# Second-group streaming in a gated attention and feed-forward block: 512-token first-layer products, tile-by-tile second layer, new call order

## The chip, the cores and the metric

The kernel runs on one core of one Trainium2 chip, in one launch. The metric is device microseconds (us). The kernel before takes 255.28 us, the median of three runs (255.18, 255.28 and 256.24). The core has a matrix engine (PE, with its weight loads shown apart as PEld), a vector engine (DVE), an activation engine (ACT), a general engine (POOL) and a queue engine (SP) that here only issues DMAs. Each engine works through its own list of instructions in order and waits on semaphores that other engines raise.

## The reference

Input x has 4 batches of 1024 tokens of 256 numbers; each batch has 154 context rows of 256. In short:

```python
xn     = layernorm(x)
scores = (xn @ Wq.T + bq) @ (ctx @ Wk.T + bk).T / 16
keep the 32 largest scores of each token, softmax over these
x  = x + tanh(g_xattn) * ((attn @ (ctx @ Wv.T + bv)) @ Wo.T + bo)
h  = relu(layernorm(x) @ W1 + b1)                # 256 -> 1024
x  = x + tanh(g_ffn) * (h @ W2 + b2)             # 1024 -> 256
```

## The kernel before, in words

Raw engine programs with semaphores written by hand. The 4096 tokens are cut into 8 groups (`GROUPS`) of 512 tokens; a group is 4 tiles of 128 tokens, and a tile pair p is two of them. Each engine has a list of calls in an order that is written out by hand (groups 0 to 2), and then a loop over g that repeats one pattern.

Setup folds Wk with Wq (`fold_queries`, `centre_queries`, `make_keys`) and Wv with Wo (`fold_values`, `values_of`), so that one product gives the scores and one the attended values. Per group and pair: `scores` (PE, plain fp32), `scale_scores` (DVE), four `topk_round` calls of eight maxima each (DVE), `exps` (ACT), `pick` (DVE), `transpose_picked` (PE), `pt_to_hi` (ACT), `pt_to_lo` (DVE), `attend` (PE), `residual` (DVE, makes x2 and its statistics), `normalise_x2` (POOL), `transpose_x2n` (PE), `x2nt_to_hi` (ACT), `x2nt_to_lo` (DVE).

The feed-forward part keeps fp32 accuracy by splitting each operand into a rounded part (hi, type fp32r) and the rest (lo), and by three fp32r products: hi by hi, hi by lo, lo by hi. Its unit is a pair: u counts the 16 pairs, c the 8 chunks of 128 of the 1024 hidden numbers.

- `ffn_in(u, c)` (lines 410 to 421): six products of 256 columns (two halves of the 256 inputs by three products) into one of two PSUM banks `z_ps`; it waits until ACT has read the chunk two before (`hid_made`).
- `relu(u, c)` (lines 741 to 748): ACT reads `z_ps` twice, once into `hid_hi` (rounded), once into `hid`; the buffers are a ring of 8 chunks of 256 tokens.
- `hid_to_lo(u, c)` (line 1279): POOL makes `hid_lo`. For the last pair DVE does that (line 1045).
- `ffn_out(u, c)` (lines 440 to 460): for both tiles of the pair two products with `hid_hi`, then for both one with `hid_lo`, each of 256 columns, summed over c in `y_ps`. Bank `y_ps[p]` holds the two tiles of pair p, so a pair's sum is opened after the output of the same pair of the group before.
- `output(g, p)` (line 1028): DVE adds 512 columns for two tiles; `add_b2` (POOL) has added the bias before. `store` sends a pair to memory.

All of PE's calls are one list in which `ffn_in` and `ffn_out` chunks stand between the attention calls of the next group. DVE's list has the top-k rounds of the next group, with outputs, residuals and conversions among them.

Of the kernel before, what the change touches and what calls it, by code (L numbers as in the profile page):

```python
# [5 lines left out]
P = 128  # L6
TILES = 4
# [5 lines left out]
RING = 8  # L13
X_RING = 3
SR = S - P
# [9 lines left out]
PARTS = [(g, t, 2) for g in range(GROUPS) for t in (0, 2)]  # L25
LAST = len(PARTS) - 1


def gated_block(nc, x, x_t, w_kq, ctx_t, w_vo, small, w1, w2, out):
# [4 lines left out]
    with stack:  # L34
# [8 lines left out]

        wkq_in = sb("wkq_in", [P, KD, 2 * (D + 1)])
        wk_in, wq_in = wkq_in[:, :, 0:D + 1], wkq_in[:, :, D + 1:2 * (D + 1)]
        ctx_in = sb("ctx_in", [P, KD, B * S])
        wvo_in = sb("wvo_in", [P, KD, 2 * D + 1])
        bk_bq = sb("bk_bq", [P, KD])
# [11 lines left out]

        hid = sb("hid", [P, RING, 2 * P])
        hid_hi = sb("hid_hi", [P, RING, 2 * P], f32r)
        hid_lo = sb("hid_lo", [P, RING, 2 * P], f32r)

        w1_in = sb("w1_in", [P, KD, F])
        w2_in = sb("w2_in", [P, KF, D])
# [28 lines left out]
        stacked = sb("stacked", [96, B - 1, D])  # L95
# [21 lines left out]
        x2 = [sb(f"x2_{i}", [P, TILES, D]) for i in range(2)]  # L117
# [3 lines left out]
        x2n = sb("x2n", [P, TILES, D])  # L121
# [56 lines left out]
        y_stored = [sem("y_stored_0"), sem("y_stored_1")]  # L178
        last_y_made = sem("last_y_made")
        last_lo_made = sem("last_lo_made")  # L180
# [4 lines left out]
        def _(sp):  # L185
# [10 lines left out]
            def store(g, p):  # L196
                sp.wait_ge(y_made, 2 * g + p + 1)
                sp.dma_start(out[g, :, 2 * p * D:2 * (p + 1) * D],
                             x2[g % 2][:, 2 * p:2 * p + 2, :].rearrange("p j d -> p (j d)")).then_inc(y_stored[p], 16)

            def store_last(t):
                sp.wait_ge(last_y_made, t + 1)
                sp.dma_start(out[GROUPS - 1, :, (2 + t) * D:(3 + t) * D], x2[(GROUPS - 1) % 2][:, 2 + t, :]).then_inc(y_stored[1], 16)
# [33 lines left out]
            sp.wait_ge(y_stored[0], 16 * GROUPS)  # L237
            sp.wait_ge(y_stored[1], 16 * (GROUPS + 1))

        @block.tensor  # L240
        def _(pe):
# [162 lines left out]
            def ffn_in(u, c):  # L404
                g, tile, tiles = PARTS[u]
                if c == 0:
                    pe.wait_ge(x2nt_lo_made, 2 * g + (tile + tiles) // 2)
                if u == 0 and c == 0:
# [5 lines left out]
                dst = z_ps[c % 2][:, 0:tiles * P]  # L414
                toks = slice(tile * P, (tile + tiles) * P)
# [7 lines left out]
            def ffn_sum(u, j):  # L423

                return sc_ps[0][:, 0:D] if u == LAST and j == TILES - 1 else y_ps[j // 2][:, (j % 2) * D:(j % 2 + 1) * D]

            def hid_hi_products(u, c, j):
                rows = slice((j - PARTS[u][1]) * P, (j - PARTS[u][1] + 1) * P)
                opens = c == 0 and (j % 2 == 0 or u == LAST)
                mm(ffn_sum(u, j), hid_hi[:, c % RING, rows], w2_hi[:, c, :], start=opens, stop=False, skip_group_check=True)  # L430
                mm(ffn_sum(u, j), hid_hi[:, c % RING, rows], w2_lo[:, c, :], start=False, stop=False, skip_group_check=True)  # L431

            def hid_lo_product(u, c, j):
                rows = slice((j - PARTS[u][1]) * P, (j - PARTS[u][1] + 1) * P)
                return mm(ffn_sum(u, j), hid_lo[:, c % RING, rows], w2_hi[:, c, :], start=False, stop=c == KF - 1, skip_group_check=True)  # L435

            def ffn_out(u, c):

                g, tile, tiles = PARTS[u]
                if c == 0:  # L440
                    if u == 0:
                        pe.wait_ge(x2_made, 2)
                    elif u == 1:
                        pe.wait_ge(vals_copied, B + 2)
                    else:
                        pe.wait_ge(y_made, 2 * (g - 1) + (tile + tiles) // 2)
                if u == 0 and c % 2 == 0:
                    pe.wait_ge(w2_lo_made, c + 2)
                pe.wait_ge(hid_hi_made, KF * u + c + 1)
                for j in range(tile, tile + tiles):  # L450
                    hid_hi_products(u, c, j)
                if u < LAST:
                    pe.wait_ge(hid_lo_made, KF * u + c + 1)
                else:
                    pe.wait_ge(last_lo_made, c + 1)
                for j in range(tile, tile + tiles):
                    last = hid_lo_product(u, c, j)
                    if c == KF - 1 and j % 2 == 1:
                        last.then_inc(ffn_made, 1)

            def last_ffn_out():

                pe.wait_ge(hid_hi_made, KF * LAST + KF)
                for j in (2, 3):
                    for c in (KF - 2, KF - 1):
                        hid_hi_products(LAST, c, j)
                        if j == 2:
                            pe.wait_ge(last_lo_made, c + 1)
                        last = hid_lo_product(LAST, c, j)
                    last.then_inc(ffn_made, 1)  # L470

            warm_up()
            fold_queries(0)
            fold_queries(1)
            fold_key_bias()
# [5 lines left out]
            fold_values(1)  # L481
            scores(0, 1)
            fold_value_bias()
            values_of(0)
            values_of(1)
            make_keys(1, 0)
            transpose_picked(0, 0)
            bias_scores(1)
            scores(1, 0)
            attend(0, 0)  # L490
            make_keys(1, 1)
            values_of(2)
            values_of(3)
            transpose_x2n(0, 0)
            values_of(4)
            scores(1, 1)
            ffn_in(0, 0)
            ffn_in(0, 1)
            values_of(5)
            transpose_picked(0, 1)  # L500
            ffn_in(0, 2)
            ffn_out(0, 0)
            ffn_in(0, 3)
            ffn_out(0, 1)
            attend(0, 1)
            ffn_in(0, 4)
            ffn_in(0, 5)
            ffn_out(0, 2)
            ffn_in(0, 6)
            ffn_out(0, 3)  # L510
            ffn_out(0, 4)
            transpose_picked(1, 0)
            transpose_x2n(0, 1)
            ffn_in(0, 7)
            scores(2, 0)
            ffn_in(1, 0)
            ffn_in(1, 1)
            attend(1, 0)
            ffn_in(1, 2)
            ffn_out(0, 5)  # L520
            ffn_in(1, 3)
            ffn_out(0, 6)
            ffn_in(1, 4)
            ffn_out(0, 7)
            ffn_out(1, 0)
            ffn_out(1, 1)
            ffn_in(1, 5)
            ffn_in(1, 6)
            transpose_x2n(1, 0)
            ffn_out(1, 2)  # L530
            ffn_out(1, 3)
            ffn_in(1, 7)
            scores(2, 1)
            transpose_picked(1, 1)
            ffn_in(2, 0)
            ffn_in(2, 1)
            ffn_out(1, 4)
            ffn_out(1, 5)
            attend(1, 1)
            ffn_in(2, 2)  # L540
            ffn_in(2, 3)
            ffn_out(1, 6)
            ffn_out(1, 7)
            ffn_in(2, 4)
            ffn_in(2, 5)
            scores(3, 0)
            ffn_out(2, 0)
            ffn_out(2, 1)
            transpose_x2n(1, 1)
            ffn_in(2, 6)  # L550
            transpose_picked(2, 0)
            ffn_in(2, 7)
            ffn_out(2, 2)
            ffn_in(3, 0)
            ffn_out(2, 3)
            ffn_out(2, 4)
            ffn_in(3, 1)
            attend(2, 0)
            ffn_in(3, 2)
            ffn_in(3, 3)  # L560
            transpose_picked(2, 1)
            ffn_out(2, 5)
            scores(3, 1)
            ffn_out(2, 6)
            ffn_out(2, 7)
            ffn_in(3, 4)
            attend(2, 1)
            ffn_in(3, 5)
            transpose_x2n(2, 0)
            ffn_out(3, 0)  # L570
# [842 lines left out]
```

## Time and profile before

| | |
|---|---|
| median of three runs | 255.28 us |
| span of the profiled execution, first to last instruction | 254.5 us |
| time around the span (median less span) | 0.8 us |
| PE, PEld, DVE, ACT, POOL busy | 249.7, 242.8, 177.6, 152.4, 171.4 us |
| PE products recorded | 2014 |
| memory read, written | 12.44, 4.19 MB |

The profile is one execution. It gives no time of its own besides its span, so the span is what sums are made against. PE products are pipelined: one of 256 columns is shown as about 0.28 us long, while the next begins about 0.12 us after it. What a product costs is the distance from its start to the next start, and a row "x8" of the timeline gives the time of eight in a run, the last one with its whole length. Idle time in square brackets is that of the engine just before the row, with what ended it.

### The profile page before, as it was taken

How to read it: one execution, taken by the hardware profiler on the slowest of the kernel's cores; microseconds unless marked ns; L12 is line 12 of the kernel's file. 1: busy time of each engine (PE TensorE's matmuls, PEld its weight loads, DVE VectorE, ACT ScalarE, POOL GpSimd, SP SyncE). 2: the span in 40 equal slices, each digit the busy share in tenths (PEclk: the TensorE clock that was granted, in tenths of full speed). 3: DMA queues.
4: the chain of work that ended last, by engine and by line, in shares of the span. 5: the costliest groups of instructions: out<-in, count | busy, mean ns of one | idle time of the engine just before them, and what ended most of it. 6: DMA issues, size and time to landing. Idle time of an engine off the chain costs nothing.

```text
span 254.5 us, 6003 instructions
## 1 busy us (share of the span) xinstructions
PE 249.7 (98%) x2014; PEld 242.8 (95%) x2014; DVE 177.6 (70%) x744; ACT 152.4 (60%) x388; POOL 171.4 (67%) x264
## 2 busy tenths in 40 slices
PE   8999999999999999999999999999999999999995
PEld 7866898999999999999999999999999999999994
DVE  2798999999996398588757794679448795421042
ACT  2576677865664755575466565675566657555652
POOL 3457996897995893569636993669456964696300
PEclk9999999999999999999999999999999999999999
DMA  7992203103312210321120211001100001001011
GB/s 223 379 416 117 66 18 107 27 3 93 115 43 85 82 43 35 91 84 45 41 85 9 76 43 45 0 3 43 43 3 0 10 34 45 1 29 56 0 44 41
DMA packets 6878, 17.30 MB, mean 68 GB/s; under 512 B 800, under 2 KB 2368, under 8 KB 6592
## 3 DMA queue, kind: packets, MB, share of 16 engines
q1 hardware_dynamic: 6848, 16.93, 19.0%
q8 instruction: 16, 0.26, 0.4%
q14 instruction: 14, 0.11, 0.1%
HBM read 12.44 MB, written 4.19 MB: 65 GB/s over the span
## 4 chain that ended last, share of the span: by engine, by line
PE 90%; DVE 6%; POOL 2%; issue 1%; ACT 0%; POOLq 0%; ACTq 0%
PE y_ps L435 11%; PE y_ps L431 11%; PE z_ps L418 11%; PE z_ps L420 11%; PE y_ps L430 11%; PE z_ps L419 11%; PE sc_ps L345 6%; PE pt_ps L366 2%; PE att_ps L400 1%; PE att_ps L387 1%; DVE left L960 1%; PE att_ps L384 1%; PE att_ps L386 1%; PE y_ps L247 1%; PE att_ps L385 1%; DVE top L956 1%
## 5 line engine op out<-in xcount | busy, mean ns | idle before, releaser
L1279 POOL TENSOR_TENSOR hid_lo<-hid,hid_hi 128x256 fp32r<-128x256 f32 x120 | 87.0, 744 | 34.6 <-ACT hid L748 33.9
L747 ACT ACTIVATE hid_hi<-z_ps,small_in 128x256 fp32r<-128x256 f32 x128 | 60.6, 473 | 70.1 <-PE z_ps L420 69.8
L418 PE MATMUL z_ps<-x2nt_hi,w_hi 128*128 128x256 f32 x256 | 73.1, 285 | 0.0
L420 PE MATMUL z_ps<-x2nt_hi,w_lo 128*128 128x256 f32 x256 | 71.5, 279 | 0.0
L419 PE MATMUL z_ps<-x2nt_lo,w_hi 128*128 128x256 f32 x256 | 71.1, 278 | 0.0
L430 PE MATMUL y_ps<-w_hi,hid_hi 128*128 128x256 f32 x248 | 66.0, 288 | 0.0
L431 PE MATMUL y_ps<-w_lo,hid_hi 128*128 128x256 f32 x248 | 64.5, 282 | 0.0
L748 ACT ACTIVATE hid<-z_ps,small_in 128x256 f32<-128x256 f32 x128 | 60.4, 472 | 0.0
L435 PE MATMUL y_ps<-w_hi,hid_lo 128*128 128x256 f32 x248 | 50.4, 282 | 0.0
L418 PEld LDWEIGHTS z_ps<-x2nt_hi,w_hi 128*128 128x128 f32 x256 | 48.3, 188 | 0.0
L419 PEld LDWEIGHTS z_ps<-x2nt_lo,w_hi 128*128 128x128 f32 x256 | 48.2, 188 | 0.0
L420 PEld LDWEIGHTS z_ps<-x2nt_hi,w_lo 128*128 128x128 f32 x256 | 48.1, 188 | 0.0
L431 PEld LDWEIGHTS y_ps<-w_lo,hid_hi 128*128 128x128 f32 x248 | 46.8, 189 | 0.0
L430 PEld LDWEIGHTS y_ps<-w_hi,hid_hi 128*128 128x128 f32 x248 | 46.8, 189 | 0.1
L435 PEld LDWEIGHTS y_ps<-w_hi,hid_lo 128*128 128x128 f32 x248 | 38.4, 189 | 0.2 <-DVE hid_lo L1045 0.2
L960 DVE MATCH_REPLACE8 left<-top,left 128x154 f32<-128x154 f32 x96 | 28.4, 304 | 0.0
L956 DVE MAX8 top<-left 128x8 f32<-128x154 f32 x96 | 25.4, 306 | 0.0
L968 DVE SCALAR_TENSOR_TENSOR picked<-left,probs 128x154 f32<-128x154 f32 x32 | 16.3, 546 | 7.4 <-ACT probs L722 7.4
L1273 POOL TENSOR_TENSOR x<-x,b_pair 128x512 f32<-128x512 f32 x16 | 20.6, 1289 | 0.0
L981 DVE SCALAR_TENSOR_TENSOR x<-att_ps,inv_denom,x_ring 128x256 f32<-128x256 f32 x31 | 13.6, 480 | 8.5 <-PE att_ps L387 8.3
L345 PE MATMUL sc_ps<-keys,xt_in 128*128 128x154 f32 x128 | 19.5, 295 | 0.0
L975 DVE TENSOR_TENSOR pt_lo<-pt_ps,pt_hi 128x256 fp32r<-128x256 f32 x16 | 6.7, 420 | 17.3 <-ACT pt_hi L735 17.3
(155 smaller groups left out, 404.2 us busy)
## 6 DMA issues: line engine op xcount, KB each, us to landing
x_ring<-x SPq DMA_DIRECT2D x8, 512.0 KB, 4.5
out<-x SPq DMA_DIRECT2D x15, 256.0 KB, 2.0
xt_in<-x_t SPq DMA_DIRECT2D x7, 512.0 KB, 3.6
w_in<-w SPq DMA_DIRECT2D x2, 1024.0 KB, 10.8
wkq_in<-w_kq SPq DMA_DIRECT2D x1, 514.0 KB, 3.4
wvo_in<-w_vo SPq DMA_DIRECT2D x1, 513.0 KB, 6.6
xt_in<-x_t SPq DMA_DIRECT2D x2, 256.0 KB, 4.9
ctx_in<-ctx_t SPq DMA_DIRECT2D x1, 462.0 KB, 10.1
```

Of the source, the lines that this page charges most:

```text
L345: last = mm(sc_ps[p][:, t * S:(t + 1) * S], xt_in[n % 2][:, k, rows], keys[:, k, at:at + S], start=k == 0, stop=k == KD - 1)
L418: mm(dst, w1_hi[:, k, cols], hi[:, k, toks], start=k == 0, stop=False)
L419: mm(dst, w1_hi[:, k, cols], lo[:, k, toks], start=False, stop=False)
L420: last = mm(dst, w1_lo[:, k, cols], hi[:, k, toks], start=False, stop=k == KD - 1)
L430: mm(ffn_sum(u, j), hid_hi[:, c % RING, rows], w2_hi[:, c, :], start=opens, stop=False, skip_group_check=True)
L431: mm(ffn_sum(u, j), hid_hi[:, c % RING, rows], w2_lo[:, c, :], start=False, stop=False, skip_group_check=True)
L435: return mm(ffn_sum(u, j), hid_lo[:, c % RING, rows], w2_hi[:, c, :], start=False, stop=c == KF - 1, skip_group_check=True)
L747: func(hid_hi[:, c % RING, :], z_ps[c % 2][:, 0:2 * P], ACT.Relu, bias=b1[:, c:c + 1]).then_inc(hid_hi_made, 1)
L748: func(hid[:, c % RING, :], z_ps[c % 2][:, 0:2 * P], ACT.Relu, bias=b1[:, c:c + 1]).then_inc(hid_made, 1)
L956: nc.vector.max(top[:, j, 8 * r:8 * r + 8], score[:, j, :] if r == 0 else left[:, j, :]).then_inc(topk_step, 1)
L960: nc.vector.match_replace(left[:, j, :], top[:, j, 8 * r:8 * r + 8], score[:, j, :] if r == 0 else left[:, j, :], TAKEN).then_inc(topk_ste ...
L1279: nc.gpsimd.tensor_tensor(hid_lo[:, slot, :], hid[:, slot, :], hid_hi[:, slot, :], ALU.subtract).then_inc(hid_lo_made, 1)
```

## The change

- Groups 0 and 1 (`PAIRED = 2`) still run `ffn_in` by pairs of 256 columns. Groups 2 to 7 run it once per chunk for the whole group, with 512 columns, into a whole bank of `z_ps`.
- `relu` and `hid_to_lo` follow: 512 columns at a time in groups 2 to 7. `hid_hi` and `hid_lo` become rings of 12 chunks of 512 tokens; `hid` is a ring of 4 chunks of 512 (or 8 halves) laid over `w1_in`.
- The second layer goes tile by tile: `ffn_out(g, t, first, last)` does the three products of 256 columns for chunks first to last-1 of one tile. Its waits on `hid_hi` and `hid_lo` stand in tile 0 alone. A tile's sum lies alone in bank `y_ps[t % 2]`, and opens after the output of the tile two before. Groups 0 and 1 use `ffn_out_pair`.
- `output(g, t)` is per tile with 256 columns. The last pair has no path of its own any more: POOL makes all of `hid_lo`.
- x2 is a ring of three, laid over `wvo_in`, `ctx_u` and `w2_in`; `x2n` is laid over `wkq_in`. `other_rests_to_lo` goes from POOL to DVE.
- Every list of calls is written out anew. At the start PE does `fold_key_bias` between `fold_queries(0)` and `fold_queries(1)`; scores and values come earlier, `make_keys(1, ...)` later. The DMA queue's list keeps its order.

```diff
-RING = 8
+RING = 12
+HID_RING = 4
+X2_RING = 3
+PAIRED = 2
+def z_index(g, c, p):
+    return 2 * KF * g + KF * p + c if g < PAIRED else KF * (g + PAIRED) + c
...
-            def ffn_in(u, c):
+            def ffn_in(g, c, p=None):
+                q = z_index(g, c, p)
...
-                if KF * u + c >= 2:
-                    pe.wait_ge(hid_made, KF * u + c - 1)
+                if q >= 2:
+                    pe.wait_ge(hid_made, q - 1)
...
+                toks = slice(0, GROUP) if p is None else slice(2 * p * P, 2 * (p + 1) * P)
+                dst = z_ps[q % 2][:, 0:toks.stop - toks.start]
...
+            def open_sum(g, t):
...
+                    pe.wait_ge(y_made, TILES * g + t - 1)
...
+            def ffn_out(g, t, first, last):
+                if first == 0:
+                    open_sum(g, t)
+                for c in range(first, last):
+                    if t == 0:
+                        pe.wait_ge(hid_hi_made, z_index(g, c, None) + 1)
+                    hid_hi_product(g, c, t)
+                    if t == 0:
+                        pe.wait_ge(hid_lo_made, z_index(g, c, None) + 1)
+                    hid_lo_product(g, c, t)
...
             warm_up()
             fold_queries(0)
+            fold_key_bias()
             fold_queries(1)
-            fold_key_bias()
             make_keys(0, 0)
...
+            ffn_in(2, 6)
+            ffn_in(2, 7)
+            ffn_out(2, 0, 1, 4)
+            attend(3, 1)
+            ffn_out(2, 1, 0, 2)
+            ffn_out(2, 0, 4, 6)
+            ffn_out(2, 1, 2, 3)
+            scores(5, 0)
+            ffn_out(2, 1, 3, 4)
+            ffn_out(2, 0, 6, 8)
+            ffn_out(2, 1, 4, 6)
+            transpose_x2n(3, 0)
+            ffn_out(2, 2, 0, 1)
+            ffn_out(2, 1, 6, 8)
+            transpose_x2n(3, 1)
+            ffn_out(2, 2, 1, 5)
...
+            ffn_in(7, 6)
+            ffn_in(7, 7)
+            ffn_out(7, 0, 1, 7)
+            ffn_out(7, 1, 0, 3)
+            ffn_out(7, 0, 7, 8)
+            ffn_out(7, 1, 3, 8)
+            ffn_out(7, 2, 0, 4)
+            ffn_out(7, 3, 0, 6)
+            ffn_out(7, 2, 4, 8)
+            ffn_out(7, 3, 6, 8)
...
+            def output(g, t):
+                dve.wait_ge(ffn_made, TILES * g + t + 1)
+                dve.wait_ge(x2b_made, 2 * g + t // 2 + 1)
+                rows = x2[g % X2_RING][:, t, :]
+                nc.vector.scalar_tensor_tensor(rows, y_ps[t % 2][:, 0:D], tanh_g[:, 1:2], rows, ALU.mult, ALU.add).then_inc(y_made, 1)
...
+            pick(4, 0)
+            residual(3, 1)
+            output(2, 0)
+            output(2, 1)
+            x2nt_to_lo(3, 0)
+            x2nt_to_lo(3, 1)
+            stats_x(5)
```

## Rows read from the trace of the kernel before

**Rows 1.** The page: busy time of each engine, then the span in 40 slices.
```profile
PE 249.7 (98%) x2014; PEld 242.8 (95%) x2014; DVE 177.6 (70%) x744; ACT 152.4 (60%) x388; POOL 171.4 (67%) x264
...
PE   8999999999999999999999999999999999999995
```

**Rows 2.** Stretches: PE, PEld, DVE, ACT, POOL busy us (instructions), granted clock, DMA.
```profile
8.60:42.00 33.40, 32.47 (x198) 26.71 (x199) 30.37 (x140) 23.95 (x60) 26.29 (x41) 1.00 0.48 183
42.00:250.00 208.00, 208.00 (x1774) 207.94 (x1774) 142.21 (x591) 126.35 (x324) 143.01 (x215) 1.00 0.13 42
```

**Rows 3.** The page: the chain that ended last, by engine.
```profile
PE 90%; DVE 6%; POOL 2%; issue 1%; ACT 0%; POOLq 0%; ACTq 0%
```

**Rows 4.** The chain in order of time: start, length; the same scores call, two groups.
```profile
126.70 1.05 PE sc_ps L345 x8
...
154.88 1.05 PE sc_ps L345 x8
```

**Rows 5.** Groups of PE instructions: busy us, mean ns of one.
```profile
L418 PE MATMUL z_ps<-x2nt_hi,w_hi 128*128 128x256 f32 x256 | 73.1, 285 | 0.0
...
L295 PE MATMUL z_ps<-wvo_in 128*128 128x256 f32 x8 | 1.9, 380 | 0.0
```

**Rows 6.** PE timeline (start, length), one first-layer chunk and the call after it.
```profile
151.13 0.28 PE L418 MATMUL z_ps<-x2nt_hi,w_hi 128*128 128x256 f32 x1
...
151.83 1.21 PE L345 MATMUL sc_ps<-keys,xt_in 128*128 128x154 f32 x8
```

**Rows 7.** PE timeline, setup: runs of products with 1 and 256 columns.
```profile
7.15 0.95 PE L261 MATMUL y_ps<-wkq_in 128*128 128x1 f32 x8
7.96 0.59 PE L264 MATMUL y_ps<-bk_bq,ones 128*128 128x1 f32 x4
...
11.54 1.89 PE L295 MATMUL z_ps<-wvo_in 128*128 128x256 f32 x8
```

**Rows 8.** PE timeline, where PE stood idle early.
```profile
16.43 1.03 PE L321 MATMUL z_ps<-wvo,first_rest 128*128 128x256 f32 x4
17.66 0.35 PE L327 MATMUL z_ps<-vo_bias_hi,ones_row 1*128 1x256 f32 x1 [0.21 <-POOL vo_bias_lo L1198]
...
26.77 0.66 PE L400 MATMUL pt_ps<-ident,x2n 128*128 128x128 f32 x4 [0.21 <-POOL x2n L1265]
...
40.77 0.60 PE L366 MATMUL pt_ps<-ident,picked 128*128 128x128 f32 x4
41.81 0.66 PE L400 MATMUL att_ps<-ident,x2n 128*128 128x128 f32 x4 [0.44 <-POOL x2n L1265]
```

**Rows 9.** DVE timeline: centring of the second half of the folded queries.
```profile
7.36 0.43 DVE L886 BATCH_NORM_STATS2 mt_stats<-z_ps 128x6 f32<-128x256 f32 x1 [0.26 <-PE z_ps L254]
...
8.44 0.15 DVE L895 COPY u_col<-z_ps 128x1 f32<-128x1 f32 x1
```

**Rows 10.** Groups on ACT, POOL and DVE: busy us, mean ns of one.
```profile
L747 ACT ACTIVATE hid_hi<-z_ps,small_in 128x256 fp32r<-128x256 f32 x128 | 60.6, 473 | 70.1 <-PE z_ps L420 69.8
...
L735 ACT ACTIVATE pt_hi<-pt_ps 128x512 fp32r<-128x512 f32 x16 | 9.6, 598 | 10.7 <-PE pt_ps L366 10.7
```

**Rows 11.** The same view, POOL.
```profile
L1279 POOL TENSOR_TENSOR hid_lo<-hid,hid_hi 128x256 fp32r<-128x256 f32 x120 | 87.0, 744 | 34.6 <-ACT hid L748 33.9 <-issue 0.3
L1273 POOL TENSOR_TENSOR x<-x,b_pair 128x512 f32<-128x512 f32 x16 | 20.6, 1289 | 0.0
```

**Rows 12.** The same view, DVE.
```profile
L956 DVE MAX8 top<-left 128x8 f32<-128x154 f32 x96 | 25.4, 306 | 0.0
L981 DVE SCALAR_TENSOR_TENSOR x<-att_ps,inv_denom,x_ring 128x256 f32<-128x256 f32 x31 | 13.6, 480 | 8.5 <-PE att_ps L387 8.3
...
L1028 DVE SCALAR_TENSOR_TENSOR x<-y_ps,tanh_g,x 128x512 f32<-128x512 f32 x15 | 11.1, 741 | 3.4 <-PE y_ps L435 3.4
```

**Rows 13.** Timeline, the end: the last product and the last output.
```profile
251.47 0.28 PE L435 MATMUL sc_ps<-w_hi,hid_lo 128*128 128x256 f32 x1
...
251.79 0.48 DVE L1036 SCALAR_TENSOR_TENSOR x<-sc_ps,tanh_g,x 128x256 f32<-128x256 f32 x1 [0.22 <-PE sc_ps L435]
```

More of the change, by code:

```diff
@@ L433, in hid_lo_product @@
[L433 to L439, printed above, removed]
-                if c == 0:
[L441 to L447, printed above, removed]
-                    pe.wait_ge(w2_lo_made, c + 2)
[L449 to L470, printed above, removed]
+            def open_sum(g, t):
+                if g == 0 and t == 0:
+                    pe.wait_ge(x2_made, 2)
+                elif g == 0 and t == 1:
+                    pe.wait_ge(vals_copied, B + 2)
+                else:
+                    pe.wait_ge(y_made, TILES * g + t - 1)
@@ L494, in _ @@
+            scores(1, 1)
+            values_of(5)
             transpose_x2n(0, 0)
[L495 to L499, printed above, removed]
-            transpose_picked(0, 1)
[L501 to L504, printed above, removed]
-            attend(0, 1)
[L506 to L510, printed above, removed]
@@ new lines, in _ @@
+            attend(5, 0)
+            ffn_in(4, 5)
+            ffn_out(4, 0, 1, 4)
+            ffn_out(4, 1, 0, 1)
+            ffn_in(4, 6)
+            ffn_in(4, 7)
+            attend(5, 1)
+            ffn_out(4, 0, 4, 5)
+            scores(7, 0)
+            ffn_out(4, 0, 5, 7)
+            ffn_out(4, 1, 1, 3)
+            ffn_out(4, 0, 7, 8)
+            ffn_out(4, 1, 3, 8)
+            transpose_x2n(5, 0)
+            ffn_out(4, 2, 0, 1)
+            ffn_out(4, 3, 0, 3)
+            transpose_x2n(5, 1)
@@ new lines, in _ @@
+            ffn_out(4, 2, 1, 3)
+            ffn_out(4, 3, 3, 5)
+            transpose_picked(6, 0)
+            ffn_in(5, 0)
+            ffn_in(5, 1)
+            scores(7, 1)
+            ffn_in(5, 2)
+            attend(6, 0)
+            ffn_in(5, 3)
+            transpose_picked(6, 1)
+            ffn_out(4, 2, 3, 8)
+            ffn_in(5, 4)
+            ffn_in(5, 5)
+            ffn_out(4, 3, 5, 7)
+            ffn_in(5, 6)
+            ffn_out(4, 3, 7, 8)
+            ffn_in(5, 7)
+            attend(6, 1)
@@ new lines, in _ @@
+            ffn_out(5, 0, 0, 1)
+            ffn_out(5, 1, 0, 1)
+            ffn_out(5, 0, 1, 3)
+            ffn_out(5, 1, 1, 2)
+            ffn_out(5, 0, 3, 4)
+            transpose_x2n(6, 0)
+            ffn_out(5, 1, 2, 3)
+            ffn_out(5, 0, 4, 8)
+            ffn_out(5, 1, 3, 8)
+            ffn_out(5, 2, 0, 5)
+            transpose_x2n(6, 1)
+            ffn_out(5, 2, 5, 6)
+            transpose_picked(7, 0)
+            ffn_out(5, 3, 0, 4)
+            ffn_in(6, 0)
+            ffn_in(6, 1)
@@ new lines, in _ @@
+            ffn_out(5, 2, 6, 8)
+            ffn_in(6, 2)
+            ffn_in(6, 3)
+            attend(7, 0)
+            ffn_in(6, 4)
+            ffn_in(6, 5)
+            ffn_out(6, 0, 0, 2)
+            ffn_in(6, 6)
+            ffn_in(6, 7)
+            ffn_out(5, 3, 4, 6)
+            transpose_picked(7, 1)
+            ffn_out(6, 0, 2, 5)
+            ffn_out(5, 3, 6, 8)
+            ffn_out(6, 0, 5, 8)
+            attend(7, 1)
+            ffn_out(6, 2, 0, 2)
+            ffn_out(6, 1, 0, 6)
@@ new lines, in _ @@
+            ffn_out(6, 2, 2, 3)
+            ffn_out(6, 1, 6, 8)
+            ffn_out(6, 2, 3, 4)
+            transpose_x2n(7, 0)
+            transpose_x2n(7, 1)
+            ffn_out(6, 3, 0, 2)
+            ffn_out(6, 2, 4, 8)
+            ffn_in(7, 0)
+            ffn_in(7, 1)
+            ffn_out(6, 3, 2, 4)
+            ffn_in(7, 2)
+            ffn_in(7, 3)
+            ffn_out(6, 3, 4, 5)
+            ffn_in(7, 4)
+            ffn_in(7, 5)
+            ffn_out(7, 0, 0, 1)
+            ffn_out(6, 3, 5, 8)
```

930 lines of the change are left out of this document (556 added, 374 removed).

## The prediction, made before the changed kernel was run

> **What bounds the kernel now.** I read the page first: PE is busy for 249.7 of 254.5 us, and its 40 slices show nines from the second on [rows 1]. A busy PE need not be a PE without waits, so the next view is the stretches: from 42 to 250 us PE and PEld are both busy all the time, 208.00 of 208.00 us, while DVE is busy 142.21, POOL 143.01 and ACT 126.35 of it [rows 2]. There no other engine makes PE wait. In 8.6 to 42 us it is otherwise: DVE is busy 30.37 of 33.40 and PE 32.47, with visible gaps [rows 2, 8]. The chain of waits says the same: 90% PE, 6% DVE [rows 3]. So the time is a short start that DVE helps to set, then the sum of PE's products by their distances, and an end of one DVE output and one store after the last product [rows 13]. A change can win by making PE's sum smaller or by removing early gaps, and lose by making PE wait in the 208 us in which it does not wait now.
>
> **The first layer at 512 columns.** Before, the feed-forward part has 16 pairs x 8 chunks x 6 = 768 first-layer products of 256 columns. Groups 2 to 7 are 12 pairs, so 576 of them become 288 of 512 columns. The 768 second-layer products stay as they are, 256 columns each.
>
> What a narrow product costs: the six of one chunk start at 151.13 and the next call at 151.83, 0.117 us each [rows 6]. A whole period checks it: the same scores call comes 28.18 us later [rows 4]. Take off two scores calls (2.10) and 16 transposes at about 0.11 (1.76); 24.32 us remain for 192 feed-forward and 16 attention products, 0.117 each. The first product after a change of call stands a little further off, and that step stays, so I take 0.116.
>
> What a wide one costs no row shows. Plain fp32 gives a slope: eight products of 154 columns take 1.05 us, 0.131 each [rows 4], and eight of 256 columns take 1.89 with the last one's 0.380 inside, 0.216 each [rows 5, 7]; that is 0.83 ns for a column and almost nothing fixed. At 1 column the distance does not go to zero: eight take 0.81 us until the next call, 0.10 each [rows 7]. So something that does not depend on columns, presumably the weight load that goes with every product, keeps products about 0.11 apart. An fp32r product of 256 columns sits just over that floor. If a column of it takes half of 0.83 ns, 256 of them need 0.107 us, the floor sets the distance, and a 512-column one takes 0.213 + 0.003 = 0.216 us with its load hidden. The bound above: the modelled lengths are 285 against 380 ns for 256 columns [rows 5], 0.37 ns per column less, so 0.46 ns a column and 0.236 us for 512, no gain at all (232 against 236 ns: a loss of 1.2 us). The bound below is 0.213 against twice 0.117, 21 ns. I take 0.216, since the half fits both the floor and the slope. Saved: 288 x (0.232 - 0.216) = 4.6 us, with ends at -1.2 and 6.0.
>
> The Trainium skill ("TensorE: Matmul & The Clock Gate", section "Back-to-back issue gap") gives an isolated distance of N/2.4 + 2.5 ns: 109.2 at 256 and 215.7 at 512. Twice 109.2 less 215.7 would save only 288 x 2.7 ns = 0.8 us, which speaks against the change. The trace disagrees at 256 fp32r columns (0.117, rows 6). By the section "LDWEIGHTS" of the same page the load of 128 columns takes P/1.2 = 107 ns, which agrees with the floor near 0.10 [rows 7]. By the first rule alone the kernel would take 254.5 us.
>
> **The second layer tile by tile.** It issues the same 768 products in the same three kinds; the waits on hid_hi and hid_lo go from three tiles of four. I cost that at nothing, between -0.5 and +0.5 us, since PE has no idle time there now [rows 2].
>
> **ACT, POOL, DVE.** A wide relu lies between 0.60 us, the 512-column copy, and two narrow ones, 0.95 [rows 10]; I take 0.65, near the copy. A wide chunk is then two of them, 1.3 us, against 6 x 0.216 = 1.30 us of PE in the same chunk plus 12 second-layer products (1.40) somewhere else. Per wide group ACT falls from 16 x 0.95 to 8 x 1.3. POOL's hid_lo goes from 0.744 at 256 to about 1.29 at 512, the time of the other two-input operation of that width [rows 11]; 8 x 1.29 = 10.3 us a group against 11.9. DVE pays for outputs: four of 256 columns (0.480, the like operation) against two of 512 (0.741) [rows 12], 0.44 us more a group, and loses eight hid_lo at the end. None of this is on PE's path while these engines have a third of their time free [rows 2]; at ACT's bound of 0.95 the two relus outlast a chunk by 0.6 us, and a third chunk in a row would wait that long for its bank. In groups 2 to 7 the list never puts more than two in a row.
>
> **The start.** `fold_key_bias` stood behind both `fold_queries`, and its 12 one-column products (7.15 to about 8.5 us) covered the centring of the second half on DVE, 7.36 to about 8.5 [rows 7, 9]. Now it comes before `fold_queries(1)`, and PE waits for the centring: about 0.9 us later scores of the first pair, and the top-k chain on DVE with it. Against it stand the early gaps. The three idle pieces are 0.21, 0.21 and 0.44 us, and with the distance before them, longer than usual, they cost about 1.3 us [rows 8]. In the new list PE has `make_keys(1, ...)`, three `values_of` and three more scores calls to do before `transpose_x2n(0, 0)`, and four second-layer chunks before `transpose_picked(1, 0)`. Going through both lists by hand with the durations above I find these three gaps filled. Net -0.4 us, between +2.1 (none filled, 0.9, and the chain a whole top-k round later, four operations of 0.3 [rows 12]) and -1.3 (all filled, the start hidden).
>
> **The end.** Group 7's hid_lo is all POOL's now. From the first product of `ffn_in(7, 0)` PE is through `ffn_in(7, 7)` after about 12.9 us (8 x 1.30, seven second-layer steps of 0.35). ACT finishes chunk 7 at 14.2, POOL at 15.5. PE wants it in `ffn_out(7, 0, 7, 8)` after nine more steps of 0.35, at 16.3: 0.8 us to spare. Then the end is as before: last product, 0.48 us output, store of one tile [rows 13]. Zero, up to +2 if the relu takes its upper bound.
>
> **Sum.** 254.5 - 4.6 - 0.4 = 249.5 us of span, and 0.8 around it, the difference between span and median: 250.3 us.
>
> **The rivals.**
> A: the extra 7 to 10 ns of a narrow product belong to its columns or to its accumulation, not to the product. Then 512 columns save 0 to 0.8 us, and the kernel takes 254.0 to 255.3; I put it at 254.6. For it: no row has fp32r at another width. Against: the floor of 0.10 at 1 column [rows 7].
>
> B, slower: the handoff of the sums. Before, a pair's bank had the time of the other pair's sums, some 14 us (half of 28.18 [rows 4]), until it was opened again. Now tile t+2 opens in the bank of tile t as soon as PE comes to it, after DVE's output. Six wide groups have four such handoffs each. The list leaves PE 1.15 us between them at the tightest (`ffn_out(2, 1, 4, 6)` and `transpose_x2n(3, 0)` before `ffn_out(2, 2, 0, 1)`). DVE needs 0.48 us, so it holds as long as DVE's queue is not over 0.6 us late there. If a residual or a top-k round (four operations of 0.3 [rows 12]) stands ahead each time, PE loses about 0.4 us at each of 24 places, 9.6 us, and the kernel takes 259.9. It decides from 5.0 / 24 = 0.21 us per handoff. For it: DVE's list is in order and holds `residual(3, 1)` right before `output(2, 0)`. Against: DVE is free for a third of the time [rows 2], and by my walk it stands waiting for PE there.
>
> C: the start does not recover, and groups 1 to 3, where DVE is at its fullest, let PE run dry: +2.1 instead of -0.4, so 252.8. For it: DVE is busy 91% of 8.6 to 42 us [rows 2]. Against: the new list does work early that stood later, scores of groups 2 and 3 among it.
>
> D: an fp32r column might stream so fast that the floor sets the wide product too, 0.116 us each; then 288 x 0.116 = 33 us would be saved, about 221.5 us. Against: 256 columns of plain fp32 take 0.216 us with loads of the same size, and streaming clearly shows there [rows 7]. The same page of the Trainium skill, in the same section, "Back-to-back issue gap", states a sustained 131 ns for 512 columns, which would make it about 226 us.
>
> **How the numbers follow.** My forecast gets 0.70, A 0.10, B 0.10, C 0.08, D 0.02. Around the forecast the wide product's distance and the start leave about 1.5 us on either side: 248.8 to 252. The range reaches up to A: 248.8 to 254.8, and leaves out B, D and a little else. This kernel's measurement can tell 0.5%, 1.3 us, from no change. The forecast, C and D are faster by more: 0.80. A is the same: 0.10. B is slower: 0.10.
>
> **What would show it.** Wide products 0.216 us apart in the timeline, 1726 products recorded (2014 - 288), a PE that is busy from some 45 us to the end, and a period of about 27.4 us per wide group (28.18 less 48 x 0.016). Distances of 0.23 would show A. Idle PE ahead of second-layer rows with DVE's output as what ended it would show B. PE gaps before 45 us of over 2 us would show C. I am wrong if the wide groups show PE waiting on ACT, or if the first scores come no later than before.

## The result: 259.26 us, slower than before and than forecast

The changed kernel takes 259.26 us, the median of four executions (258.42, 258.51, 260.01 and 263.47), against 255.53 for the kernel before (255.28 in its first three). The ratio to before is 1.0123, interval 1.0093 to 1.0152: 1.2% slower, where the forecast was 250.3 us, faster. Medians here are over all executions of a kernel, ratios over those within 1.5% of its fastest. The profiled execution took 258.42 us, with a span of 256.6, so 1.8 us lie around a span.

The page with its chain, and the stretches (columns as in [rows 2]), of the changed kernel, against [rows 1 to 3]:

```profile
PE 249.8 (97%) x1726; PEld 230.3 (90%) x1726; DVE 177.3 (69%) x752; ACT 136.0 (53%) x292; POOL 168.5 (66%) x223
...
PE 95%; DVE 2%; issue 1%; ACT 0%; POOL 0%; POOLq 0%
```
```profile
8.60:42.00 33.40, 31.70 (x196) 26.87 (x197) 31.39 (x143) 22.70 (x56) 25.66 (x38) 1.00 0.45 175
42.00:250.00 208.00, 207.72 (x1469) 193.94 (x1468) 142.66 (x599) 110.80 (x230) 140.72 (x177) 1.00 0.13 44
```

PE has 288 products fewer and is busy just as long. From 42 to 250 us it stands for 0.28 us of 208, once, for POOL, so the time went into the products themselves. The PE timeline (start, length) shows them, six wide products of one chunk and the second layer behind them:

```profile
148.58 0.39 PE L428 MATMUL z_ps<-x2nt_hi,w_lo 128*128 128x512 f32 x1
148.81 0.39 PE L426 MATMUL z_ps<-x2nt_hi,w_hi 128*128 128x512 f32 x1
...
149.98 0.39 PE L428 MATMUL z_ps<-x2nt_hi,w_lo 128*128 128x512 f32 x1
150.21 0.28 PE L442 MATMUL y_ps<-w_hi,hid_hi 128*128 128x256 f32 x1
```

From 148.81 to 150.21 six wide products take 1.40 us, 0.233 each: twice the 0.117 of [rows 6]. I add up, over each whole timeline, the distance from every product's start to the next start:

| us | before | after | e15 (below) |
|---|---|---|---|
| first layer | 90.32 | 91.85 | 91.46 |
| of it, groups 0 and 1 (192 narrow) | 22.86 | 24.07 | 23.87 |
| of it, groups 2 to 7 (576 narrow; 288 wide) | 67.46 | 67.78 | 67.59 |
| second layer, 768 products | 93.04 | 94.24 | 91.40 |
| all other products | 67.08 | 66.27 | 65.91 |
| start of the last product | 251.47 | 253.39 | 249.80 |

The wide products cost 67.78 / 288 = 0.2353 us with the steps between calls, and 0.32 us more in all than the 576 narrow ones that they replace. The 1.21 us that groups 0 and 1 lost are no price of a product: their sum holds a wait for a pick (from 32.83 to 34.11 us, below). The second layer lost 1.20 us. "Other" hides a loss: in the profiled execution of before, eight 257-column products of the setup took 3.13 us, while the same eight took 1.30 and 1.11 after, so that execution began some 0.7 us late, and it is the 256.24 one of the three (254.5 + 1.8). Against an execution of before that did not begin late, the start lost more. PE's waits (waiting for whom, us, times, longest) and the start in its timeline:

```profile
PE pt_ps L285 <- issue: 1.3, 1, 1.3
...
PE pt_ps L374 <- DVE picked L1144: 1.0, 1, 1.0
```
```profile
6.66 1.11 PE L262 MATMUL z_ps<-wkq_in 128*128 128x257 f32 x4
9.08 0.76 PE L285 MATMUL pt_ps<-ctx_in,mt 128*128 128x154 f32 x4 [1.31 <-issue]
...
32.83 0.28 PE L428 MATMUL z_ps<-x2nt_hi,w_lo 128*128 128x256 f32 x1
34.11 0.76 PE L374 MATMUL pt_ps<-ident,picked 128*128 128x128 f32 x4 [1.01 <-DVE picked L1144]
```

Of the early gaps [rows 8] the small ones went, but PE now stands for 1.31 us ahead of L285, until the second half is centred (the view names no releaser; e4 below takes the wait away), and for 1.01 us until the second pick.

### The profile page after: what moved, and what is told of

It is laid out like the page before. It is cut to its first block, busy times and chain, and to the rows that moved or that the text cites. A ratio compares the mean times of both kernels' runs of the same rounds, so it can differ in the third digit from the quotient of the medians.

```text
span 256.6 us, 5207 instructions
## 1 busy us (share of the span) xinstructions
PE 249.8 (97%) x1726; PEld 230.3 (90%) x1726; DVE 177.3 (69%) x752; ACT 136.0 (53%) x292; POOL 168.5 (66%) x223
## 4 chain that ended last, share of the span: by engine, by line
PE 95%; DVE 2%; issue 1%; ACT 0%; POOL 0%; POOLq 0%
PE y_ps L442 12%; PE y_ps L447 12%; PE y_ps L443 12%; PE z_ps L426 11%; PE z_ps L428 11%; PE z_ps L427 11%; PE sc_ps L353 6%; PE pt_ps L374 3%; PE att_ps L408 1%; PE att_ps L395 1%; PE att_ps L394 1%; PE att_ps L392 1%; PE att_ps L393 1%; PE z_ps L329 1%; PE y_ps L255 1%; PE z_ps L285 1%
## 5 line engine op out<-in xcount | busy, mean ns | idle before, releaser
L1519 POOL TENSOR_TENSOR hid_lo<-w_in,hid_hi 128x512 fp32r<-128x512 f32 (+1 forms) x80 | 85.1, 1076 | 46.6 <-ACT w_in L872 45.0
L871 ACT ACTIVATE hid_hi<-z_ps,small_in 128x512 fp32r<-128x512 f32 (+1 forms) x80 | 48.1, 601 | 46.4 <-PE z_ps L428 44.4
L426 PE MATMUL z_ps<-x2nt_hi,w_hi 128*128 128x512 f32 (+1 forms) x160 | 56.9, 356 | 0.0
L427 PE MATMUL z_ps<-x2nt_lo,w_hi 128*128 128x512 f32 (+1 forms) x160 | 55.7, 348 | 0.0
L428 PE MATMUL z_ps<-x2nt_hi,w_lo 128*128 128x512 f32 (+1 forms) x160 | 55.6, 348 | 0.0
L872 ACT ACTIVATE w_in<-z_ps,small_in 128x512 f32<-128x512 f32 (+1 forms) x80 | 47.8, 598 | 0.0
L428 PEld LDWEIGHTS z_ps<-x2nt_hi,w_lo 128*128 128x128 f32 x160 | 30.0, 188 | 4.4
L427 PEld LDWEIGHTS z_ps<-x2nt_lo,w_hi 128*128 128x128 f32 x160 | 30.2, 189 | 3.1
L426 PEld LDWEIGHTS z_ps<-x2nt_hi,w_hi 128*128 128x128 f32 x160 | 30.1, 188 | 3.1
L353 PEld LDWEIGHTS sc_ps<-keys,xt_in 128*128 128x128 f32 x128 | 17.4, 190 | 0.9 <-ACT keys L787 0.5
```

The costliest lines, as they stand in the source:

```text
L353: last = mm(sc_ps[p][:, t * S:(t + 1) * S], xt_in[n % 2][:, k, rows], keys[:, k, at:at + S], start=k == 0, stop=k == KD - 1)
L871: func(hid_hi[:, slot, toks], z, ACT.Relu, bias=b1[:, c:c + 1]).then_inc(hid_hi_made, 1)
L872: func(plain, z, ACT.Relu, bias=b1[:, c:c + 1]).then_inc(hid_made, 1)
L1519: nc.gpsimd.tensor_tensor(hid_lo[:, slot, toks], plain, hid_hi[:, slot, toks], ALU.subtract).then_inc(hid_lo_made, 1)
```

## Experiments

Ratios are to the kernel before on the same chip. Where no other edit is named, a kernel is the changed one.

**e1 and e2: one product by itself.** Kernels of their own; the whole computation is left out, and PE only runs series of products with the same operand types. In outline:

```diff
+for c in range(8):                      # e1: 128, 256, 384, 512 columns
+    for k in range(KD):
+        mm(dst, w1_hi[:, k, cols], x_hi[:, k, 0:N], ...)   # hi hi, hi lo, lo hi
+for w_at, x_at in PLACES:               # e2: where weights and moving operand begin
+    wide(w_at, x_at); narrow(w_at, x_at)
```


> A kernel that leaves the block's computation out: after its loads and splits PE runs twelve segments of 48 products each (plain fp32 16) with nothing beside them, of 128, 256, 384 and 512 columns, and only the last segment has ACT, DVE and POOL busy beside it. Theory W (a wide fp32r product costs twice a narrow one by itself: streaming at about 0.455 ns a column): 256 columns 0.114 to 0.117 us apart, 384 columns 0.175, 512 columns 0.233, the same with zero data and with nothing beside it; bf16 at 512 columns 0.216. Rival L (0.216 is right, and the changed kernel's other engines slow the wide product): 512 columns 0.216 alone and 0.233 in the last segment only. Rival Z (the data slow it): 0.216 with zeros, 0.233 with x. Rival S (the sum in the bank slows it): 0.216 where every product starts its own sum. For the second layer: by tile 0.120 and by pair 0.1175 if the order of the products makes the difference, equal if it was the buffers' places.

The distances of fp32r products: 0.111 us at 128 columns, 0.120 at 256, 0.173 at 384, 0.227 at 512. Zero data, products that aren't summed, and other engines at work left 0.227 as it was, so rivals L, Z and S fall, while W's 0.233 isn't reached either. The order falls as a cause in the second layer: by pair and by tile its products were 0.120 us apart. From 256 to 512 a column takes (227 - 120) / 256 = 0.418 ns; what is left, 227 - 512 x 0.418 = 13 ns, comes with every product. In the same run bf16 at 512 columns took 0.216 and plain fp32 at 256 took 0.216. The Trainium skill, "TensorE: Matmul & The Clock Gate", section "Back-to-back issue gap", gives about 216 ns at 512 columns (N/2.4 + 2.5): bf16 agrees with it, fp32r doesn't.

> A kernel that leaves the block's computation out: runs of 12 fp32r products of 512 and of 256 columns at 24 pairs of places of the two operands (weights 0 to 448 bytes further, moving columns 0 to 1536 bytes further), with nothing beside them. Theory P (what a product pays above its columns depends on where its operands lie against each other): the wide distance moves between about 0.220 and 0.234 us and the narrow one between 0.113 and 0.120 from place to place. Rival F (a fixed cost for fp32r, the same anywhere): 0.227 and 0.120 at all 24 places; then the 0.233 and 0.114 of the changed kernel come from what runs beside its products.

The distance depends on where the operands begin in a partition, and mostly on the difference of weights' and moving operand's address modulo 256 bytes. The timeline of e2, weights 256 bytes on (difference 0), then 320 (difference 64), each first wide, then narrow:

```profile
99.99 0.40 PE L82 MATMUL z_ps<-x_lo,w_hi 128*128 128x512 f32 x1
...
102.27 0.39 PE L82 MATMUL z_ps<-x_lo,w_hi 128*128 128x512 f32 x1
...
102.72 0.28 PE L87 MATMUL z_ps<-x_lo,w_hi 128*128 128x256 f32 x1
...
103.92 0.28 PE L87 MATMUL z_ps<-x_lo,w_hi 128*128 128x256 f32 x1
...
104.39 0.40 PE L82 MATMUL z_ps<-x_lo,w_hi 128*128 128x512 f32 x1
...
106.72 0.40 PE L82 MATMUL z_ps<-x_lo,w_hi 128*128 128x512 f32 x1
...
107.19 0.28 PE L87 MATMUL z_ps<-x_lo,w_hi 128*128 128x256 f32 x1
...
108.33 0.28 PE L87 MATMUL z_ps<-x_lo,w_hi 128*128 128x256 f32 x1
```

Ten steps each: 0.228 wide and 0.120 narrow at 0 bytes, 0.233 and 0.114 at 64. At 32 bytes it was 0.233 and 0.118. The difference isn't all: at other pairs of places with a difference of 0 the wide products were up to 0.231 apart, and at 64 the narrow ones up to 0.116. Nor does the split of e1 hold everywhere: at 64 bytes the same two widths give (233 - 114) / 256 = 0.46 ns a column and nothing that comes with every product. Why the place matters stays open.

Both kernels have w1 64 bytes from x2n's transpose. hid stood 32 bytes from w2 before and 0 after; the commonest distance of the second layer went from 117 to 120 ns. The best wide product (0.228) is worth two of the best narrow ones (0.114): each at its best place, width doesn't win.

**e3: wide products in halves.** Relu, hid_lo and the lists stay wide.

```diff
-mm(dst, w1_hi[:, k, cols], hi[:, k, toks], start=k == 0, stop=False)
 ...
+for w, m in ((w1_hi, hi), (w1_hi, lo), (w1_lo, hi)):
+    for h in range((toks.stop - toks.start) // half):
+        part = slice(toks.start + h * half, toks.start + (h + 1) * half)
+        last = mm(dst[:, h * half:(h + 1) * half], w[:, k, cols], m[:, k, part], ...)
```


> The changed kernel with each first-layer product of 512 columns issued as two of 256, all else as it is. If a wide product saves nothing over two narrow ones in this kernel (0.2335 against 2 x 0.1144 us), the time falls by 288 x 0.0047 = 1.4 us: span of a fast run 255.3 us, ratio to before about 1.007. If narrow products cost 0.120 here, as they did alone, the time rises by 288 x 0.0065 = 1.9 us, ratio 1.020. If the forecast's wide product (0.216) had held and something else had eaten it, it would rise by 288 x 0.016 = 4.6 us.

The first layer fell to 90.42 us, by 1.43. The time hardly did: 257.05 to 262.10 us, 1.0115 [1.0079, 1.0150]. In its profiled execution (259.07 us) PE runs at 1.2 GHz, the lower of its two clocks, for some 3 us right behind the 1.31 us wait at L285, and the other products took 68.35 instead of 66.27. The page's clock, and two stretches with their granted clock (third number from the end):

```profile
PEclk9799999999999999999999999999999999999999
```
```profile
10.00:11.00 1.00, 1.00 (x5) 1.00 (x6) 1.00 (x5) 0.00 (x0) 0.00 (x0) 0.50 1.10 449
11.00:12.00 1.00, 1.00 (x5) 1.00 (x5) 0.99 (x6) 0.39 (x1) 0.59 (x2) 0.50 1.02 430
```

That would hide the gain: the one execution with a mean granted clock of 1.0 took 257.05 us, 1.4 below the changed kernel's best.

**e4: the start as before.**

```diff
 fold_queries(0)
+fold_queries(1)
 fold_key_bias()
-fold_queries(1)
```
with `copy_key_bias` behind `centre_first_queries` on ACT.

> The changed kernel with fold_key_bias behind both fold_queries again on PE, and copy_key_bias behind centre_first_queries on ACT. If the start costs what the trace shows (PE idle 1.31 us ahead of make_keys), the time falls by about 0.9 us, ratio 1.009, and the 1.0 us that PE waits for pick at 33 us stays. If the start is made up later, the time stays at 1.012 and the wait at 33 us grows or the PE gap shows elsewhere.

257.52 us, 1.0067 [1.0046, 1.0087]. The wait at L285 is gone and "other" fell to 65.27, by 1.0 us. The wait for the pick stayed (1.0). The mean granted clock was 0.998 or more in all six executions, so the fall behind the wait, which e3, e5 and e7 show in their traces and the changed kernel's trace doesn't, went with it.

**e5: second layer, two chunks at a time** (the waits are left out of the cut).

```diff
-for c in range(first, last):
-    hid_hi_product(g, c, t)
-    hid_lo_product(g, c, t)
+for c in range(first, last, 2):
+    both = range(c, min(c + 2, last))
+    for d in both: hid_hi_product(g, d, t)
+    for d in both: hid_lo_product(g, d, t)
```

> The changed kernel with the second layer's products of one tile in the order hi hi hi hi lo lo over two chunks in place of hi hi lo for each, in groups 2 to 7. If the order sets the distance (0.1175 between hi products in pairs against 0.120 in the tile order), 576 products get 1.1 ns less on average, 0.6 us, ratio 1.010. If the places of the buffers set it, 1.012 as before.

94.24 became 93.99 us; 258.44 to 263.34 us, 1.0136 [1.0096, 1.0176]. The order of the three products is not it.

**e6, e7: places.** 192 bytes behind hid_lo make hid less w2 64 bytes (e6); 64 bytes ahead of x2nt make w1 less x2nt 0 (e7).

```diff
+sb("gap", [P, 48])      # e6
+sb("x_gap", [P, 16])    # e7
```


> The changed kernel with 192 unused bytes behind hid_lo, so that hid_hi and hid_lo lie 64 bytes (modulo 256) from w2 and not 0. Theory P (the place of weights against moving columns, modulo 256 bytes, sets a product's distance, as in the run of places: 0.1198 at 0 bytes, 0.114 to 0.1156 at 64): the second layer's products come down from 0.120 to about 0.115 us, 768 x 0.0045 = 3.5 us, a span near 253.2 us, ratio about 0.999. Rival F (the second layer is slower for its order or for what runs beside it): still 0.120, ratio 1.012.

e6: the second layer's distances fell from 119.4 to 115.5 ns (means from 80 to 170 us, without those over 150 ns). The twelve executions took 256.00 to 265.06 us, 1.0063 [1.0038, 1.0088], a gain like that of e4. The profiled one is that of 265.06: there PE waits 3.9 us for an output on DVE, which e10 explains.

> The changed kernel with 64 unused bytes ahead of x2nt, so that w1 lies 0 bytes (modulo 256) from x2nt and not 64. Theory P: a wide product falls from 0.2335 to 0.2277 us and a narrow one of groups 0 and 1 rises from 0.1144 to 0.1197: 288 x 0.0058 less and 192 x 0.0053 more, 0.7 us less in all, ratio about 1.010. Rival F: 0.2335 and 0.1144 stay.

e7: wide from 233.8 to 229.2 ns, narrow from 115.5 to 119.9 (without those over 260 and 150 ns), the first layer 91.35 us (0.5 less); 1.0150 [1.0124, 1.0176], no gain in the time. Five of six executions had a mean granted clock of 0.993, the profiled one with its fall behind the same wait as in e3; the sixth took 257.81 us, 0.6 below the changed kernel's best.

**e8: e4, e6 and e7 together**, and `transpose_picked(0, 1)` (PE) and `copy_rest(0, 1)` (ACT) later in their lists, for the wait at L374.

```diff
-transpose_picked(0, 1)
 ...
+transpose_picked(0, 1)
```

> The changed kernel with the places of both runs above, fold_key_bias and copy_key_bias back behind fold_queries and centre_first_queries, and transpose_picked(0, 1) on PE and copy_rest(0, 1) on ACT moved behind the third and the second chunk. Theory P with the start as measured: 3.5 us from the second layer, 0.7 from the first, 1.4 from the start, up to 1.0 from the wait for pick: 6 us less than the changed kernel, ratio about 0.989, faster than both kernels. Rival F: the start and the wait alone, ratio about 1.003.

255.09 us, 0.9974 [0.9963, 0.9985], where 0.989 was expected; six executions took 254.49 to 255.26 us, two 261.38 and 261.78.

**e9: the kernel before with hid 64 bytes from w2.**

```diff
+sb("gap", [P, 8])       # ahead of hid
+sb("gap_2", [P, 56])    # behind hid_lo
```

> The kernel before with 32 unused bytes ahead of hid and 224 behind hid_lo, so that hid_hi and hid_lo lie 64 bytes (modulo 256) from w2 and not 32; nothing else is changed. Theory P: the second layer's products fall from 0.118 us (32 bytes: 0.1179 in the run of places) to about 0.115, 768 x 0.0035 = 2.7 us, ratio about 0.990. Rival F: 1.000.

No gain: 1.0012 [0.9999, 1.0025]. The second layer fell by 0.67 us and the first rose by 1.28 (distances under 150 ns from 115.4 to 117.0), though w1 and x2nt kept their difference. So the difference of e2 is not all of it; what else counts stays open.

**e10 and e11: e8 without e7's gap**, wide products in halves as in e3 (e10) or whole (e11).

```diff
-sb("x_gap", [P, 16])
```

> The changed kernel with the start of e4, the two transposes of pick moved, the second layer's operands 64 bytes apart (as in e6), the first layer's left at 64 bytes, and every wide product issued as two of 256 columns (as in e3). If the effects measured one by one add up: 258.5 us of the undisturbed changed kernel less 1.4 (halves), 2.5 (second layer's place), 1.0 (start) and about 0.6 for the moved transposes: 253 to 254 us, ratio about 0.993, below both kernels; first layer near 90.0 us of distances, second layer near 89. Rival: moving hid_hi and hid_lo spoils the first layer by 2 ns a product as it did in e9 (768 x 2 ns = 1.5 us): about 255.2, no better than e8.

> The same kernel as e10 with the wide products left whole. Against e10 it tells what width alone costs where narrow products have their best place: 288 x (232.5 - 2 x 114.5) = 1.0 us more than e10, so 254 to 255 us. If a wide product saves anything (the forecast's 0.216 us), it would be 288 x (229 - 216) = 3.7 us faster than e10. If width is free, equal to e10.

e10: 258.68 us, 1.0121 [1.0076, 1.0167], some 5 us above the 253 to 254 of the single effects. e11: two executions took 254.87 and 255.24 us, four 259.97 to 261.76, so no ratio. The timeline of e10 shows where:

```profile
185.29 6.38 POOL L1523 TENSOR_TENSOR hid_lo<-w_in,hid_hi 128x512 fp32r<-128x512 f32 x5
186.66 3.88 DVE L1148 SCALAR_TENSOR_TENSOR picked<-left,probs 128x154 f32<-128x154 f32 x1
...
190.48 1.37 DVE L1148 SCALAR_TENSOR_TENSOR picked<-left,probs 128x154 f32<-128x154 f32 x1
...
191.98 0.48 DVE L1208 SCALAR_TENSOR_TENSOR ctx_u<-y_ps,tanh_g,ctx_u 128x256 f32<-128x256 f32 x1
192.52 0.39 PE L446 MATMUL y_ps<-w_hi,hid_hi 128*128 128x256 f32 x1 [2.42 <-DVE ctx_u L1208]
```

A pick (0.31 us alone) takes 3.88, as long as three of POOL's operations; `output(4, 3)` stands behind it on DVE, and PE waits for that before it opens the next sum. Then PE runs at 1.2 GHz (granted 0.51, the stretches of e10):

```profile
192.90:195.60 2.70, 2.70 (x16) 2.70 (x15) 2.70 (x15) 0.00 (x0) 0.08 (x1) 0.51 0.25 97
```

**e12, e13, e14: output(4, 3) ahead of pick(7, 0)**, in e11, the changed kernel and e10.

```diff
-pick(7, 0)
 output(4, 3)
+pick(7, 0)
```


> e11 with one pair of lines of DVE's list swapped: output(4, 3) now comes before pick(7, 0). Theory: pick(7, 0), two DVE operations with two operands in SBUF, can be held up while POOL runs its hid_lo operations back to back (3.88 us in e10's trace and 6.37 us in e6's, against 0.31 alone), and output(4, 3) stands behind it, for which PE waits before it opens tile 1 of group 5 (2.4 and 3.9 us). Then with the swap no execution loses that: all executions at 254.8 to 255.5 us, none of 258 and above, ratio 0.997 to 0.999. Rival: the long executions have another cause (a slow start, or PE's clock by itself); then about half of them stay at 258 to 262 us.

> The changed kernel as it is, with only the same swap. Theory: the executions of 263 us go; what is left is 258.4 and, where PE's clock is low in the first slices, 260.0; ratio 1.011 to 1.017, since the wide products, the second layer's place and the start are untouched. Rival: if the handoff of the sums (rival B of the forecast) makes most of the loss in every execution, the swap gives back over 1 us in all of them: 257.5 or less.

> e10 (wide products in halves) with the same swap. If halves save 288 x (232.6 - 2 x 115.5) = 0.5 us against e12 and e10 lost its time to the wait alone: 254.3 to 255 us, ratio 0.995 to 0.998. If halves cost something else (twice as many instructions on PE's queue): slower than e12 by 1 us or more.

e12: 258.31 us, 1.0082 [1.0057, 1.0106], all six from 257.25 to 258.80. The theory's cure failed: the pick took 5.27 us beside four of POOL's operations, and PE waited 2.0 for a later output behind it.

```profile
PE y_ps L443 <- DVE w_in L1205: 2.0, 1, 2.0
```
```profile
188.41 5.27 DVE L1145 SCALAR_TENSOR_TENSOR picked<-left,probs 128x154 f32<-128x154 f32 x1
```
e13: 258.99 us, 1.0092 [1.0057, 1.0126]; its best executions (257.68 to 258.12) are 0.3 to 0.7 us below the changed kernel's best, so the handoff isn't what the changed kernel loses in all of them. The theory had expected executions like the changed kernel's 263.47 to go; two stayed (263.05 and 263.46). The trace of e13 is the one of 263.46, and it lost its time elsewhere, in the setup:

```profile
6.01 1.71 PE L269 MATMUL y_ps<-wkq_in 128*128 128x1 f32 x8
7.58 0.99 PE L272 MATMUL y_ps<-bk_bq,ones 128*128 128x1 f32 x4
...
11.80 1.37 PE L285 MATMUL pt_ps<-ctx_in,mt 128*128 128x154 f32 x4 [1.31 <-issue]
...
39.25 0.76 PE L374 MATMUL pt_ps<-ident,picked 128*128 128x128 f32 x4 [0.99 <-DVE picked L1144]
```

Eight one-column products take 1.57 us to the next call, against 0.81 in the changed kernel's trace, though the granted clock is shown as 1.00 there, and L374 comes at 39.25 in place of 34.11 us. That is the whole loss: the last product starts 5.04 us later. Why the setup ran so stays open, and the changed kernel's own 263.47 left no trace.

e14: 257.62 us, 1.0072 [1.0043, 1.0100].

**e15, e16: POOL lets the pick in**, in e11 and e10.

```diff
 hid_to_lo(5, 4)
+pool.wait_ge(picked_made, 4 * 7 + 2)
 hid_to_lo(5, 5)
```


> e11 (start mended, second layer's operands 64 bytes apart, wide products) with one wait added on POOL: before the hid_lo of chunk 5 of group 5 it waits until pick(7, 0) is done, so that DVE's two operations with two SBUF operands get in after at most one POOL operation (about 1.3 us each, as in e11's trace) and not after three to five (3.9 to 6.4 us). Theory (POOL's back-to-back operations hold the pick, the pick holds output(4, 3), that holds PE): every execution at 254.8 to 255.6 us, none above 257, ratio 0.997 to 0.999. Rival: the long executions come from something else, and stay at 258 to 262 us as in e11.

> e10 (the same with wide products in halves) with the same wait on POOL. Theory: 0.5 us below e15, 254.3 to 255.1 us, ratio 0.995 to 0.997, and no execution above 257. Rival: halves cost what they save (their second-layer products were 1 to 2 ns further apart in e10 and e14 than in e11): 255 to 256 us, no better than e15.

e15: 254.45 us, 0.9955 [0.9939, 0.9971], all seven executions from 253.84 to 254.96. The timeline of e15: the picks take 1.38 and 0.31, and POOL stands 0.50 us.

```profile
184.63 3.83 POOL L1520 TENSOR_TENSOR hid_lo<-w_in,hid_hi 128x512 fp32r<-128x512 f32 x3
187.25 1.38 DVE L1145 SCALAR_TENSOR_TENSOR picked<-left,probs 128x154 f32<-128x154 f32 x1
...
188.56 0.31 DVE L1145 SCALAR_TENSOR_TENSOR picked<-left,probs 128x154 f32<-128x154 f32 x1
...
188.96 3.82 POOL L1520 TENSOR_TENSOR hid_lo<-w_in,hid_hi 128x512 fp32r<-128x512 f32 x3 [0.50 <-ACT w_in L873]
```

So POOL's row of operations held the pick. The same pick took 1.38 and 1.41 us in e11's execution of 254.87, so POOL holds it long in some executions only; that e15 has none of them was measured on another chip than e11, but e16 fell against e10 in the same way. e15 is 0.45% below the kernel before. e16: 254.59 us, 0.9965 [0.9948, 0.9982]: halves are no better than whole products here (first layer 90.87 against 91.46, second 91.92 against 91.40), so this gain isn't one of width.

The Trainium skill, "SBUF — State Buffer", section "SBUF: two separate sides", says that a DVE operation with two SBUF inputs and a GpSimd operation that reads SBUF exclude each other for a whole instruction. The traces agree (a pick of 0.31 us takes 1.38 beside POOL in e15), and add that one pick can wait out several POOL operations in a row (3.88 us in e10).

## Why the prediction was wrong, step by step

- **"I take 0.216, since the half fits both the floor and the slope."** This step failed, and it is most of the error. At the places of e1 the half was right, 0.42 ns a column against half of 0.83, but an fp32r product adds 13 ns, not 3, which makes 0.227; at the kernel's places it is 0.2335. The narrow products, at 0.117, did not sit on a floor that hid anything: in e1 the distance grows by the same 0.42 ns a column from 256 to 384 and from 384 to 512. Instead of 4.6 us saved, the wide products take 0.32 more than the narrow ones they replace: 4.9 us of the error. That is the place of rival A (no gain from width; I gave it 0.10), and the bound of 0.236, worked out from the lengths of [rows 5], was the right end. Of A's reasons the accumulation falls (products that aren't summed stayed at 0.227 in e1). A's 254.6 us was still too low, for the losses below.
- **The second layer, "I cost that at nothing, between -0.5 and +0.5 us".** It cost 1.20. The order is innocent (e5: 0.25; e1: 0.120 either way). The new layout moved hid against w2, from 32 to 0 bytes, and the distances under 150 ns rose from 118.3 to 119.3 ns, about 0.8 us of the loss; e6 shows that distance following the place. The rest lies in longer steps. I looked at what PE does and not at where the buffers lie.
- **The start, "I find these three gaps filled. Net -0.4 us".** They went, but waits of 1.31 and 1.01 us came. "Other" shows -0.8, beside an execution of before that began late, and groups 0 and 1, with the wait for the pick, +1.2: +0.4 in all; e4 gives 1.0 back. C's direction, without its size. The first scores start at 10.84 us against 10.39, later by 0.45 where I had 0.9.
- **"0.8 around it".** It is 1.8: I set the span of one execution against the median of others.
- **ACT, POOL, the end: right.** A wide relu takes 0.688 and 0.681 us (forecast 0.65), hid_lo 1.299 (1.29):

```profile
L871 ACT ACTIVATE hid_hi<-z_ps,small_in 128x512 fp32r<-128x512 f32 x48 | 33.0, 688 | 36.0 <-PE z_ps L428 34.0
L872 ACT ACTIVATE w_in<-z_ps,small_in 128x512 f32<-128x512 f32 x48 | 32.7, 681 | 0.0
...
L1519 POOL TENSOR_TENSOR hid_lo<-w_in,hid_hi 128x512 fp32r<-128x512 f32 x48 | 61.8, 1299 | 42.0 <-ACT w_in L872 40.7
```
  What follows the last product's start takes 3.2 us against 3.0. The working of the end has a slip: nine steps of 0.35 after 12.9 us lead to 16.0, not 16.3, and leave 0.5 us to spare, not 0.8; PE did not wait there.
- **Rival B** doesn't show in the changed kernel's trace. Its mechanism is real: in e6, e10 and e12 one handoff costs 3.9, 2.4 and 2.0 us, at a place where "by my walk it stands waiting for PE there" held only as long as POOL let the pick through. I had not looked at which DVE operations POOL can hold up.

The sum: 250.3 + 4.9 (wide products) + 1.2 (second layer) + 0.8 (start) + 1.0 (around) + 0.2 (end) = 258.4, the profiled execution.

## What to carry to other kernels

Price a product of a new width from that type's own distance at two widths, or bound it by both and let the range go to the end where nothing is saved; a modelled length is evidence too. Where PE waits for nobody, a buffer that moves is an edit: compare the operands' addresses before and after. Where a sum's bank gets less slack, look at what else is queued ahead of the output, and which other engine's work can stretch that.

## What the runs showed of the hardware that was not expected

- At the places of e1 fp32r products cost 0.42 ns a column and 13 ns each; bf16 at 512 columns had 0.216 us, 11 ns less than fp32r (e1).
- The places of weights and moving operand in the partition move a distance between 0.114 and 0.120 us at 256 columns and 0.228 and 0.234 at 512 (e2); in e6 the second layer's went from 119.4 to 115.5 ns, by an estimate 768 x 3.9 ns = 3 us. e9 doesn't follow the places wholly.
- A DVE operation of 0.31 us took 3.88 and 5.27 us beside POOL's (e10, e12).
- After 2.42 us of waiting PE was granted 0.51 of its clock for the next 2.7 us, though it was busy throughout (e10); after 1.31 us it was granted 0.50 for some 3 us in e3, and 1.00 in the changed kernel's trace.
- Setup products stood nearly twice as far apart in one execution as in another, with a granted clock of 1.00 in both (eight in 1.57 us in e13, in 0.81 in the changed kernel's trace).
